# Three instructions moved in the queues of GpSimd, VectorE and ScalarE of a fused graph network kernel

## The reference

```
h  = relu(layernorm(x))
sj = (h Wv + bv) aw[:256];  si = (h Wv + bv) aw[256:]
alpha = A * exp(leaky_relu(sj[None, :] + si[:, None] + ab, 0.2))
T  = alpha / (rowsum(alpha) + 1e-12)
x1 = x + relu(h Wk0 + T h Wk1 + T T h Wk2 + sum of bk)
h1 = relu(layernorm(x1))
y0 = relu(A h1 W1 + b1);  y1 = relu(A y0 W2 + b2)
out = x1 + A y1 W3 + b3
```

## Time and profile before

| what | value |
|---|---|
| median of 3 runs | 866.6 us (865.77 to 868.97) |
| the profiled execution: time, span | 867.2 us, 865.4 us |
| TensorE busy (weight loads) | 846.4 us, 98% (794.7 us, 92%) |
| VectorE busy | 728.3 us, 84% |
| ScalarE busy | 683.7 us, 79% |
| GpSimd busy | 509.3 us, 59% |
| granted TensorE clock | 0.996 of full speed |

### The profile page before, as it was taken

The page is one execution under the profiler, slowest core; times in us unless marked ns, Lnnn a source line. Parts: engine busy times, 40 slices in busy tenths (PEclk is TensorE's granted clock), DMA queues, the critical chain, the costliest instruction groups (busy, mean ns, idle before and its releaser), DMA issues.

```text
span 865.4 us, 21032 instructions
## 1 busy us (share of the span) xinstructions
PE 846.4 (98%) x6236; PEld 794.7 (92%) x6236; DVE 728.3 (84%) x2001; ACT 683.7 (79%) x1671; POOL 509.3 (59%) x593
## 2 busy tenths in 40 slices
PE   6899999999999999999999999999999999999996
PEld 5799999999999999999999999999999999999995
DVE  4788888888888888888888888888888888888872
ACT  4688888888888888888888887887888888888773
POOL 3555655655655655665665665665665665665652
PEclk9999999999999999999999999999999999999999
DMA  8153343343343443443343344334334334334101
GB/s 201 35 119 80 98 99 84 97 97 82 99 97 81 101 95 82 100 96 87 96 95 91 93 94 94 89 94 93 91 94 98 87 92 100 84 94 99 45 25 37
DMA packets 245488, 78.19 MB, mean 90 GB/s; under 512 B 202368, under 2 KB 237312, under 8 KB 245376
## 3 DMA queue, kind: packets, MB, share of 16 engines
q1 hardware_dynamic: 244288, 75.81, 37.2%
q10 hardware_dynamic: 1088, 1.05, 0.4%
HBM read 44.04 MB, written 32.77 MB: 89 GB/s over the span
## 4 chain that ended last, share of the span: by engine, by line
PE 94%; DMA 1%; POOL 1%; issue 1%; DVE 1%; ACT 1%; SPq 0%; ACTq 0%; DVEq 0%; POOLq 0%
PE bank L950 45%; PE bank_p L950 35%; PE bank_turned L950 7%; PE bank_T L950 5%; PE bank_T L971 2%; DMA w_raw<-in_L_gnn_Wk 1%; POOL w_gcn_lo L420 0%; DMA h_blocks<-h_rows 0%; PE bank_p L1127 0%; POOL w_p_lo L415 0%; POOL rstd L376 0%; SPq L307 0%; SPq L286 0%; DVE y_full L767 0%; ACT y_full L604 0%
## 5 line engine op out<-in xcount | busy, mean ns | idle before, releaser
L385 POOL TENSOR_TENSOR y__lo<-y_full,y__hi 128x256 fp32r<-128x256 f32 x256 | 183.3, 736 | 159.6 <-ACT y_full L604 159.6
L376 POOL TENSOR_TENSOR rstd<-veps,minus_half 128x2 f32<-128x2 f32 x128 | 111.5, 871 | 180.2 <-DVE veps L682 174.0
L950 PE MATMUL bank_p<-w_p_hi,h0T_hi 128*128 128x258 f32 (+1 forms) x512 | 175.7, 359 | 1.0 <-ACT h0T_hi L502 0.7
L950 PE MATMUL bank_p<-w_p_lo,h0T_hi 128*128 128x258 f32 (+1 forms) x512 | 165.0, 338 | 0.0
L950 PE MATMUL bank_p<-w_p_hi,h0T_lo 128*128 128x258 f32 (+1 forms) x512 | 141.8, 338 | 0.0
L950 PE MATMUL bank<-w_gcn_hi,y__hi 128*128 128x256 f32 x512 | 130.9, 291 | 1.6 <-ACT y__hi L604 1.3
L950 PE MATMUL bank<-w_gcn_lo,y__hi 128*128 128x256 f32 x512 | 124.7, 279 | 0.0
L604 ACT ACTIVATE y__hi<-bank,bias_col 128x256 fp32r<-128x256 f32 x256 | 119.6, 467 | 3.0 <-PE bank L950 3.0
L604 ACT ACTIVATE y_full<-bank,bias_col 128x256 f32<-128x256 f32 x256 | 120.4, 470 | 0.0
L950 PEld LDWEIGHTS bank_p<-w_p_hi,h0T_hi 128*128 128x128 f32 x512 | 96.6, 189 | 7.1 <-ACT h0T_hi L502 0.9
L950 PEld LDWEIGHTS bank_p<-w_p_lo,h0T_hi 128*128 128x128 f32 x512 | 96.8, 189 | 5.8
(11 more groups left out here) (95 smaller groups left out, 2300.2 us busy)
## 6 DMA issues: line engine op xcount, KB each, us to landing
x_in<-in_x SPq DMA_DIRECT2D x64, 256.0 KB, 3.1
x_new<-x_out SPq DMA_DIRECT2D x64, 256.0 KB, 2.2
h_rows<-h SPq DMA_DIRECT2D x61, 256.0 KB, 2.0
h_blocks<-h_rows SPq DMA_DIRECT2D x244, 64.0 KB, 2.5
adj_blocks<-in_adj SPq DMA_DIRECT2D x256, 32.0 KB, 2.0
w_raw<-in_L_gnn_Wk ACTq DMA_DIRECT2D x3, 256.0 KB, 7.1
w_raw<-in_L_gnn_W SPq DMA_DIRECT2D x3, 256.0 KB, 6.2
bk_bc<-in_L_gnn_bk SPq DMA_DIRECT2D x1, 384.0 KB, 5.9
```

The costliest lines, as they stand in the source:

```text
L376: pool.tensor_tensor(rstd[n][k % 2][:], veps[n][k % 2][:], minus_half[:], ALU.pow)\
L385: pool.tensor_tensor(y[n][1][:, c], y_full[n][:, c], plain(y[n][0][:, c]), ALU.subtract)\
L950: return pe.matmul(dst, stationary, moving, start=start, stop=stop, skip_group_check=True)
```

## The change

Three edits of order; no instruction is added or removed.

- GpSimd: `adjT_low` leaves the end of step i for pair i and stands in step i + 1, behind `power(1, b)`, for the same pair (then pair b).
- VectorE: `p2_low` leaves the middle of x1's `moments` and stands behind `guard_variance`. `turn_adj` is made for the next pair, behind `finish`; only step 1 still turns its own pair in the old place. `attention` stands behind `shift` instead of ahead of it.
- ScalarE: `norm(b)` stands ahead of `aT_high(a)`.

```diff
--- before.py
+++ after.py
@@ -442,6 +442,7 @@
                     y_low(0, c, k - LAG_C)
                 if b is not None:
                     power(1, b, k - LAG_B)
+                    adjT_low(b, (k - LAG_B) % ROUND)
                 if (n := LATE_NORMS.get(i)) is not None:
                     power(0, n, n)
                 if first(i):
@@ -454,8 +455,6 @@
                     out_bias(b, (k - LAG_B) % ROUND)
                 if (n := late_moments(i)) is not None:
                     power(0, n, n)
-                if (n := here(i, 0)) is not None:
-                    adjT_low(n, k)
                 if first(i):
                     gcn_weights_low()
 
@@ -628,10 +627,10 @@
                 if a is not None:
                     exponentials(a, k)
                     p1_copy(a, k, 0)
-                if a is not None:
-                    aT_high(a, k)
                 if b is not None:
                     norm(b, kb)
+                if a is not None:
+                    aT_high(a, k)
                 if c is not None:
                     layer_result(1, c)
                 if a is not None:
@@ -897,16 +896,16 @@
                     h_sum(b, kb)
                     residual(b, kb)
                     x1_statistics(b, kb)
-                    moments(1, b, kb, lambda: p2_low(a, k) if a is not None else None)
+                    moments(1, b, kb, lambda: None)
                     guard_variance(1, b, kb)
-                elif a is not None:
+                if a is not None:
                     p2_low(a, k)
-                if a is not None:
+                if second(i):
                     turn_adj(a, k)
-                if a is not None:
-                    attention(a, k)
                 if b is not None:
                     shift(1, b, kb)
+                if a is not None:
+                    attention(a, k)
                 if i == 1:
                     x_statistics(3, 3)
                     moments(0, 3, 3, lambda: None)
@@ -917,6 +916,8 @@
                     aT_low(a, k)
                 if d is not None:
                     finish(d, kd)
+                if nxt is not None:
+                    turn_adj(nxt, kn)
                 if i == 1:
                     shift(0, 3, 3)
                 if a is not None:
```

More of the change, by code:

```diff
@@ L630, in one @@
                     p1_copy(a, k, 0)
+                if b is not None:
+                    norm(b, kb)
                 if a is not None:
                     aT_high(a, k)
-                if b is not None:
-                    norm(b, kb)
                 if c is not None:
@@ L899, in one @@
                     x1_statistics(b, kb)
-                    moments(1, b, kb, lambda: p2_low(a, k) if a is not None else None)
+                    moments(1, b, kb, lambda: None)
                     guard_variance(1, b, kb)
-                elif a is not None:
+                if a is not None:
                     p2_low(a, k)
-                if a is not None:
+                if second(i):
                     turn_adj(a, k)
+                if b is not None:
+                    shift(1, b, kb)
                 if a is not None:
                     attention(a, k)
-                if b is not None:
-                    shift(1, b, kb)
                 if i == 1:
```

## The result

The changed kernel takes 843.54 us (median of 4 runs, 842.66 to 844.44), the kernel before beside it 866.88 (4 runs): ratio 0.9728, 95% interval 0.9707 to 0.975. By the 866.6 us of the earlier runs that is 843.0 us. By the same 866.6 us the interval of the ratio is 841.2 to 844.9 us. The profiled execution took 843.8 us with a span of 842.0 and a granted clock of 0.995.

A forecast was written before the change was run, and what follows sets the result against it. TensorE was taken as the bound, with 0.38 us a step of waits to give back; less 0.04 at aT_hi, 0.34 a step, 19.7 us over 58 steps plus 0.1 for step 62, gave 846.8 us, range 843.5 to 856.

The forecast's parts named there:

- new wait: TensorE at aT_hi's second load: the norm now runs ahead of aT_hi, costing 0.04 us a step.
- s2 wait: TensorE at y's low-part load for s2, blamed on GpSimd's order: 0.24 us to be gained in step 30.
- s3's wait: TensorE at y's low-part load for s3, blamed on ScalarE's lateness: gone, both low-part waits together 0.38 us a step.
- start and tail: The time outside the steady steps: its change was taken as nothing.
- Part 1: GpSimd: adjT_low behind rstd of x1 saves 0.24 us at s2's low-part load; VectorE's residual takes 0.69 instead of 0.94.
- Part 2: VectorE: p2_low behind veps, adjacency turned a step ahead; rstd of x1 taken as 0.70 us beside p2_low.
- Part 3: ScalarE: norm ahead of aT's high part; layer 1's results start 0.60 us earlier, the wait at s3's low part goes.
- rival C: GpSimd's rstd is slow beside p2_low, 1.07 us: 1.7 us slower, 868.3 us; chance 0.05.
- pessimistic count: VectorE's m_lo would end at 413.29 to 413.36, a possible TensorE wait of 0 to 0.2 us, taken as 0.
- Rival D: VectorE's shift is held behind GpSimd's adjT_lo: 20 us slower, 886.9 us; chance 0.09, shared with other waits over 0.45 us.
- A: Only the GpSimd edit pays; a later aT_hi or m_lo's wait takes back s3's gain: 853.8 us; chance 0.21.
- B: No wait at all on TensorE, the 0.04 us at aT_hi is not paid: 844.5 us; chance 0.08.

The follow-up runs named there:

- split norm: The changed kernel with aT_high placed between the norms of the two graphs on ScalarE: 841.89 us, ratio 0.9694; run once more, 841.06 us, ratio 0.9682.
- part 1 alone: The kernel before with only GpSimd's adjT_low moved behind rstd of x1: 855.92 us, ratio 0.9862.
- part 3 alone: The kernel before with only ScalarE's norm put ahead of aT_high: 893.06 us, ratio 1.0284.
- parts 1 and 2: The kernel before with the GpSimd and VectorE edits, ScalarE's order left as it was: 870.14 us, ratio 1.0022.
- parts 2 and 3: The changed kernel with the GpSimd edit taken back, adjT_low in its old place: 852.55 us, ratio 0.9812.

## Why it came out as it did

**The step that failed** is in the first part of the prediction: "That is all that TensorE can be given back: 58 x 0.38 = 22 us." Idle time drawn in front of loads was taken for all the time that a step could lose, and the sum then took 0.04 us a step off it for the new wait: 19.7 us. In these 58 steps TensorE was given back 22.5 us (750.5 to 728.0), and that after paying for the new wait. The loads themselves also ran closer together, and the new wait was priced too high. A step became 0.387 us shorter where the prediction had 0.34. In order along the step, as means of the 58 steps:

- *Up to aT_hi's loads*: 0.188 us less. The s2 wait gives back 0.20, of which 0.02 is lost again in the products p0 and p1. In step 30 the prediction read 0.24.
- *aT_hi*: a wait of 0.015 instead of 0.04. The chain was right: aT_hi ends at 8.14 after the step's start, and 409.18 - 401.02 = 8.16 was forecast. So was the delayed second load, 8.30 against 8.31. What was off is where that load would stand without a wait: at 8.29 in the kernel with the split norm, not at 409.29 - 401.02 = 8.27. Of a wait that is the difference of two such numbers, 0.02 is half.
- *s3's wait*: 0.18 us less. Both waits together gave 0.37 net, against a forecast of 0.38.
- *z1's loads and s3's low part*: 0.03 us less, a term that the prediction does not have. z1's loads stand 113.5 ns or some 118 ns apart, for the whole of z1. The slower spacing is there in 32 of 60 steps before and in 4 after. What sets it stays open.

So the mis-sized terms are the new wait (0.025 a step, 1.5 us) and the missing spacing of z1 (0.03 a step, 1.7 us), less 0.6 us for what the two waits gave short of 0.38. With the loads in between and unrounded that is 2.8 of the 3.6 us that separate the forecast span, 845.6, from 842.0. The other 0.8 lies outside the 58 steps, where the prediction took "start and tail" as nothing: step 4 starts at 63.79 instead of 64.46, step 62 lasts 12.56 instead of the 12.62 forecast, and from step 63 to the end it is 37.6 instead of 37.7. Of the 0.67 ahead of step 4, step 3 gave 0.26, which the sum had left out. The other 0.41, from the start to step 3, is within chance: in the two traces of the split norm, which are one kernel, step 3 starts at 52.27 and at 50.63. It is nearly as large as the 0.5 us by which the kernel came out below the range.

**Part 1** did what was said, in the changed kernel and alone. y's low parts for s2 follow rstd, and the residual takes 0.69 instead of 0.94 as GpSimd is idle beside it.

**Part 2** did too. rstd of x1 starts 0.85 us earlier, as forecast for both parts together: some 0.2 of it is part 1's shorter residual, and 0.61 is p2_low's. rstd takes 0.69 beside p2_low, so rival C (1.07) is refuted. Moving the transpose gave little: back in its old place it costs 0.03 us a step in the changed kernel, nothing with the norm split. Moving alpha behind the shift was not tried by itself.

**Part 3** gave layer 1's results 0.61 us earlier (0.60 forecast) and removed s3's wait. m_lo ends at 11.84 into the step; the prediction's pessimistic count, 413.29 to 413.36 or 12.3, did not come true, and taking its wait as 0 was right for the reason given: VectorE had been waiting for ScalarE, not working.

**Rival D** is refuted in step 30: the shift, 396.50 to 396.84, runs at 0.34 inside adjT_lo, 396.43 to 397.17. The Trainium skill ("VectorE: DVE Perf Modes", Mode 2×_2P — use both read ports for one tensor) has a float32 tensor_scalar in SBUF take both read ports. By the rule that the prediction drew from it, the shift would have been held and the time rival D's, about 887 us; the trace disagrees for this one-column form. alpha, with two SBUF inputs, is held: 0.69 instead of 0.42, and it ends 0.27 behind adjT_lo. That alpha would be delayed and cost nothing was forecast, and so it came.

**A and B.** A's 853.8 is the time of part 1 alone. B, no wait at all and 844.5 us, was nearer to what happened than the forecast itself: the wait at aT_hi is 0.015 us. But B's sum has the same ceiling of 0.38 a step, and the kernel came out below it too.

**No part can be priced by itself.** In steps: part 1 alone -0.18 us, part 3 alone +0.39, parts 1 and 2 +0.06, all three -0.38. Part 2 loses until ScalarE's order lets the norm use it, and part 3 loses until part 2 has made the shift early.

The version that beats both kernels is the split norm: 841.1 to 841.9 us. No load of its step is drawn with a wait, and the step took 12.527 us in all three traces of such a kernel, so I expect no more from another order on the other engines; what is left to shorten is TensorE's own work. That expectation was not tested.

## What to carry to other kernels

Where the critical engine waits at two places of a loop for two different engines, find for each wait the instruction that stands in the queue without being needed there, and move the whole group together: here one single move gave 1.4%, another cost 2.8%, and the set gave 2.7%. Where an engine runs two instructions for two consumers and one is double (a norm of two graphs), try the urgent single one between the halves before choosing which goes first; here that was worth 0.025 us a step. In this kernel a load that stood 0.23 us ahead of the next one could come 0.12 us late for nothing, as the next then followed after 0.11, so read the cost of a wait at the next load and not at the one that shows the idle time.

## What the runs showed of the hardware that was not expected

**The same loads have two spacings.** TensorE's loads of z1 in the kernel before, step 29 and then step 30; their operands and shapes are the same:

```profile
400.11 0.19 PEld L950 LDWEIGHTS bank<-m_hi,w_gcn_hi 128*128 128x128 f32 x1
400.23 0.19 PEld L950 LDWEIGHTS bank<-m_hi,w_gcn_lo 128*128 128x128 f32 x1
400.34 0.19 PEld L950 LDWEIGHTS bank<-m_hi,w_gcn_hi 128*128 128x128 f32 x1
...
400.57 0.53 PEld L950 LDWEIGHTS bank<-m_lo,w_gcn_hi 128*128 128x128 f32 x4
...
413.05 0.19 PEld L950 LDWEIGHTS bank<-m_hi,w_gcn_hi 128*128 128x128 f32 x1
413.17 0.19 PEld L950 LDWEIGHTS bank<-m_hi,w_gcn_lo 128*128 128x128 f32 x1
413.28 0.19 PEld L950 LDWEIGHTS bank<-m_hi,w_gcn_hi 128*128 128x128 f32 x1
...
413.52 0.54 PEld L950 LDWEIGHTS bank<-m_lo,w_gcn_hi 128*128 128x128 f32 x4
```

From the fifth of the twelve loads to the next step's start it is 401.02 - 400.11 = 0.91 us in the one and 413.99 - 413.05 = 0.94 in the other. The three kernels with a wait ahead of s3's low part have the slow spacing in 32, 35 and 49 of 60 steps; the ones without it in 0 to 15. A wait shortly before goes with it, but it is not the whole cause, since the changed kernel showed 4 slow steps in one trace and 14 in the next. Nor does it always begin in the same place. In the kernel before, 31 of the 32 slow steps have s3's high part at 113 ns and turn slow behind the wait; in the second trace of the changed kernel, 13 of the 14 are slow in s3's high part already. The granted clock is 1.00 (2.4 GHz) from 400 to 800 us in these traces, so it is not the clock. What sets the spacing stays open.

**VectorE's veps (two columns) is held beside a GpSimd instruction, its one-column shift is not.** In the kernel before, x1b on GpSimd lasts until 400.42 + 1.31 = 401.73, and veps of x's norm (128x2) stretches to just behind it:

```profile
400.42 1.31 POOL L395 TENSOR_TENSOR x1b<-x,bias_out 128x512 f32<-128x512 f32 x1
...
401.48 0.28 DVE L682 TENSOR_SCALAR veps<-mv 128x2 f32<-128x2 f32 x1
```

In the changed kernel GpSimd gets to x1b sooner, since y's low parts come sooner, and veps takes its bare time:

```profile
389.31 1.31 POOL L395 TENSOR_TENSOR x1b<-x,bias_out 128x512 f32<-128x512 f32 x1
...
390.59 0.17 DVE L681 TENSOR_SCALAR veps<-mv 128x2 f32<-128x2 f32 x1
```

In the kernel with the norm split (first trace) x1b ends between these two:

```profile
389.81 1.31 POOL L395 TENSOR_TENSOR x1b<-x,bias_out 128x512 f32<-128x512 f32 x1
...
390.95 0.20 DVE L685 TENSOR_SCALAR veps<-mv 128x2 f32<-128x2 f32 x1
```

In both kernels veps ends 0.03 us behind x1b, in each of the 58 places where the two overlap: it takes 0.28 us in the mean in the kernel before, 0.20 in the split norm, and 0.17 in either without x1b beside it. So it is held, and not slow for another reason. The aggregation just ahead of it (mv, 128x2) takes 0.16 us a piece beside x1b and without it, and the shift (128x1) 0.21 either way. In the kernel of parts 2 and 3, where veps is not held, rstd starts 0.71 into the step instead of 0.79. That this is what shrinks the s2 wait there is read from the traces; no run separated it.
